# Another order of the same steps in the per-turn programs of four engines, in a transformer block pipelined over sequence groups

## The chip, the cores and the metric

One core of one Trainium2 chip runs the whole model as one program. The metric is the device time of one execution in microseconds (us). TensorE (PE), VectorE (DVE), ScalarE (ACT) and GpSimd (POOL) each run their own instruction stream in its written order, SyncE (SP) issues the transfers, and semaphores tie the five together.

## The reference

The input x is 32 sequences of 64 tokens with 256 features; a context of the same shape goes with it. Four layers follow each other: L0, a small attention over channels; L1 and L2, transformer layers; L3, a recurrence with a gated feed-forward part. The change lies in the program of L1 and L2. Cut to what matters, one of these two layers is:

```python
def layer(x, enc, self_mask, cross_mask, ...):         # x: (32, 64, 256), 16 heads of 16
    h = layernorm(x, ln1_s, ln1_b)
    q, k, v = split_heads(h @ w_qkv + b_qkv)
    x = x + merge(attention(q, k, v, self_mask)) @ w_ao + b_ao
    h = layernorm(x, ln2_s, ln2_b)
    q = split_heads(h @ w_q + b_q);  k, v = split_heads(enc @ w_kv + b_kv)
    x = x + merge(attention(q, k, v, cross_mask)) @ w_co + b_co
    h = layernorm(x, ln3_s, ln3_b)
    return x + gelu(h @ w1 + b1) @ w2 + b2             # w1: 256x1024

def attention(q, k, v, mask):
    s = einsum(q, k) / 4 * mask - 10000 * (1 - mask)
    return einsum(softmax(s), v)
```

## The kernel before

The program has three phases, one after the other: `phase_a` computes L0, `phase_b` L1 and L2, `phase_c` L3. Everything is float32. The 2048 tokens are cut into 4 groups of 512 tokens (8 sequences), and a group into 4 tiles of 128 tokens (2 sequences on the 128 partitions).

`phase_b` is a software pipeline of 8 turns (2 layers x 4 groups), numbered 0 to 7. A turn n has 8 slots: slots 0 to 3 do the self attention of the 4 tiles of group n, slots 4 to 7 their cross attention. Spread over the slots of the same turn lie two more jobs: the MLP of the group before (`prev`), and the first layer norm and the q, k, v projections of the group after (`nxt`). Turn 0 has no `prev`, turn 7 has no `nxt`; turns 1 to 6 have all three and run as a hardware loop. Each engine has a hand-written function `turn(n, prev, nxt)` that lists its steps in order; a step is a small function that first waits for semaphores and then issues its instructions. An engine never runs a later step before an earlier one.

The path of one attention tile k is: `scores` (PE, line 780), `mask` (DVE, 1172: multiply), `add_mask` (POOL, 632), `maximum` (DVE, 1179), `subtract` (DVE, 1184), `exps` (ACT, 1018), `probs_T` (PE, 788: transposes), `copy_pT` (ACT, 1023), `times_v` (PE, 803), `normalize` (DVE, 1190 and 1192), `result_T` (PE, 811), `copy_cT` (ACT, 1028), `out_project` (PE, 824), `residual` (DVE, 1201 to 1208: add, statistics), `inv_std` (POOL, 637), `norm` (DVE, 1213). In slot k an engine works at several tiles: `scores` and `mask` are two tiles ahead, `maximum`, `subtract` and `exps` one tile ahead, `out_project`, `residual` and `norm` one tile behind.

The self-attended tile then becomes a cross query: `norm_T_mid` (PE, 711), `norm_out_mid` (ACT, 995), `queries_mid` (PE, 761) and its copy, also named `queries_mid` (ACT, 1005). In slots 1 to 4 `out_project` of the next tile waits for that copy, for the PSUM bank is the same.

The MLP of `prev`: `norm_T_mlp` (PE, 722), `norm_out(2)` (ACT, 987), eight times `hidden` (PE, 838) with `pre` (DVE, 1226), two `gelu` of 4 chunks each (ACT, 1034), four `mlp_out` (PE, 850) with `result` (DVE, 1220). `hidden` j waits for `pre` j-2, as there are two banks; `gelu(prev, 0)` waits for `pre` 3, `gelu(prev, 1)` for `pre` 7. `norm_T_mlp` waits for the second `values(1)`.

The entry of `nxt`: `stats_in` (DVE, 1135 to 1142), `inv_std_in` (POOL, 641), `norm_in` (DVE, 1148: subtract the mean, times 1/std; this is the centring), `norm_T_in` (PE, 705; it also waits for `pre` 5), `norm_out(0)` (ACT, 987), `queries_in`, `keys_in` (PE, 683; ACT, 1000 and 1011), `values_in` (PE, 693; DVE `values(0)`, 1155). The context keys and values of group n itself are `keys_ctx`, `values_ctx` (PE, 683 and 693), with `keys(1)` on ACT (1011) and `values(1)` on DVE (1155). `keys_ctx` 0 also waits for `ready["middle"]`, which SP gives once the weights of the layer are there; in turn 4 these are the ones of L2. `add_bias` (POOL, 619 and 625) and `add_bias_in` (POOL, 611) add bias rows to the residual stream.

Of the kernel before, what the change touches and what calls it, by code (L numbers as in the profile page):

```python
# [425 lines left out]
def phase_b(nc, io, ps, w, x_mid, ld_b, ld_c, ld_set, zero_ok, a_stored, b_loads, stored, c_loads):  # L426

    ctx = ExitStack()
    with ctx:
# [172 lines left out]
        def _(pool):  # L602
# [3 lines left out]

# [32 lines left out]
            def inv_std_in(n):  # L639
                pool.wait_ge(in_var_ok, NP * n + NP)  # L640
                pool.tensor_tensor(rstd_in[:, :], var_in[:, :], minus_half[:, :], ALU.pow).then_inc(in_rstd_ok, 1)

            def turn(n, prev, nxt):
                for k in range(TILES):
                    if k >= 1:
                        inv_std(n, k - 1)
                    elif prev is not None:
                        inv_std(prev, TILES - 1)
                    if nxt is not None and k == 1:
                        inv_std_in(nxt)  # L650
                    if k + 2 < TILES:
                        add_mask(n, k + 2)
                    elif nxt is not None:
                        add_mask(nxt, k + 2 - TILES)
                    if k >= 2:
                        add_bias(n, k - 2)
                    elif prev is not None:
                        add_bias(prev, TILES - 2 + k)
                    if nxt is not None and 2 <= k < 2 + NP:
                        add_bias_in(nxt, k - 2)  # L660
# [15 lines left out]
        def _(pe):  # L676
# [20 lines left out]
            def norm_T_in(n, prev):  # L697
                if prev is not None:
# [155 lines left out]
            def begin(n, k, prev):  # L854
                probs_T(n, k)
# [5 lines left out]
            def middle(n, k, nxt):  # L861
                times_v(n, k)
# [5 lines left out]
            def end(n, k):  # L868
                if 1 <= k < 1 + NP:
                    norm_T_mid(n, k - 1)  # L870
                result_T(n, k)

            def turn(n, prev, nxt):
                mlp, more = prev is not None, nxt is not None

                begin(n, 0, prev)
                keys_ctx(n, 0, prev)
                middle(n, 0, nxt)
                keys_ctx(n, 1, prev)
                end(n, 0)  # L880
                values_ctx(n, 0)

                begin(n, 1, prev)
                values_ctx(n, 1)
                middle(n, 1, nxt)
                if mlp:
                    norm_T_mlp(prev, n)
                end(n, 1)
                if mlp:
                    hidden(prev, 0)  # L890
                queries_mid(n, 0)

                begin(n, 2, prev)
# [1275 lines left out]
```

## Time and profile before

| | |
|---|---|
| median of 3 runs | 1296.84 us (1296.36 to 1297.08) |
| the profiled execution | 1294.62 us, span 1292.8 us |
| mean granted TensorE clock | 0.952 |
| busy shares of the span | PE 88%, PEld 54%, DVE 67%, ACT 42%, POOL 33% |
| turns of `phase_b` | from 146.0 us (first `probs_T`) to about 861 us |

The span runs from the first to the last instruction. "Idle before" is the time in which an engine did nothing before an instruction, and the name after the arrow is what ended it. A timeline row gives the start, the length, the engine and line, what it writes and reads, and how many instructions are merged in it. The ends of matmuls are modelled, so that a start taken from one row to the next is surer than an end.

### The profile page before, as it was taken

What the parts mean: (1) busy time and instruction counts of PE and PEld (TensorE: products, weight loads), DVE (VectorE), ACT (ScalarE), POOL (GpSimd) and SP (SyncE); (2) the same over time, 40 slices, a digit from 0 to 9 for tenths busy, and PEclk for the clock granted to TensorE, in tenths of its full rate; (3) what the DMA queues carried; (4) which work ended last, traced back from release to release, by engine and by line L of the source; (5) the groups of instructions that cost most, each with busy time, mean ns of one, the idle gap of its engine ahead of it and who ended that gap; (6) DMA issues with size and microseconds to landing.
All of it is one profiled execution on the core that took longest, in us unless ns stands there. A gap on an engine that the chain in (4) does not pass through costs nothing. (4 is left out here: it accounts for less than half of the span.)

```text
span 1292.8 us, 21232 instructions
## 1 busy us (share of the span) xinstructions
PE 1138.4 (88%) x7808; PEld 702.2 (54%) x7808; DVE 872.5 (67%) x1613; ACT 541.0 (42%) x1003; POOL 425.3 (33%) x387
## 2 busy tenths in 40 slices
PE   6985777999999999899899999887898998989976
PEld 4662555667658667567577576665232433523414
DVE  4993676776866866867767767722368686695664
ACT  3552444463564473463564554521213314214222
POOL 2111243343332333342433432410245353263240
PEclk9997889999999999999999999989699998998987
DMA  7120000001002010103001000300000010000100
GB/s 231 57 94 28 5 18 17 22 1 34 20 0 65 20 57 16 32 16 102 0 16 37 0 0 17 121 17 25 24 1 19 1 34 17 8 27 1 33 0 17
DMA packets 37150, 40.51 MB, mean 31 GB/s; under 512 B 8032, under 2 KB 32608, under 8 KB 36848
## 3 DMA queue, kind: packets, MB, share of 16 engines
q1 hardware_dynamic: 36976, 39.81, 9.5%
q8 instruction: 27, 0.44, 0.1%
q14 instruction: 19, 0.16, 0.0%
q0 software_dynamic: 128, 0.10, 0.0%
HBM read 31.52 MB, written 8.39 MB: 31 GB/s over the span
## 5 line engine op out<-in xcount | busy, mean ns | idle before, releaser
L1179 DVE TENSOR_REDUCE b_neg_max<-b_sc 128x16 f32<-128x1024 f32 x64 | 77.8, 1216 | 84.2 <-POOL b_sc L632 83.7
L838 PE MATMUL ps<-b_hT_mlp,wl 128*128 128x512 f32 x256 | 124.5, 614 | 9.9 <-ACT b_hT_mlp L987 8.8
L850 PE MATMUL ps<-w,b_act_g 128*128 128x256 f32 x512 | 119.9, 389 | 6.0 <-ACT b_act_g L1034 5.5
L637 POOL TENSOR_TENSOR b_rstd<-b_var,b_minus_half 128x1 f32<-128x1 f32 x64 | 35.1, 548 | 260.0 <-DVE b_var L1208 260.0
L1538 POOL TENSOR_TENSOR c_rs<-c_st,c_rF 128x512 f32<-128x512 f32 x64 | 82.0, 1284 | 107.7 <-DVE c_st L1956 107.7
L632 POOL TENSOR_TENSOR b_sc<-b_sc,b_self_add 128x1024 f32<-128x1024 f32 x32 | 75.8, 2368 | 104.7 <-DVE b_sc L1172 104.7
L850 PEld LDWEIGHTS ps<-w,b_act_g 128*128 128x128 f32 x512 | 96.8, 194 | 24.5 <-ACT b_act_g L1034 6.4
L1018 ACT ACTIVATE b_sc<-b_sc 128x1024 f32<-128x1024 f32 x64 | 67.9, 1062 | 93.9 <-DVE b_sc L1184 93.3
L632 POOL TENSOR_TENSOR b_sc<-b_sc,b_cross_add 128x1024 f32<-128x1024 f32 x32 | 75.5, 2359 | 82.6 <-DVE b_sc L1172 82.6
L1023 ACT ACTIVATE b_pT<-ps 128x512 f32<-128x512 f32 x128 | 70.2, 604 | 64.1 <-PE ps L788 64.1
L1184 DVE TENSOR_TENSOR b_sc<-b_sc,b_neg_max 128x1024 f32<-128x1024 f32 x64 | 79.2, 1238 | 1.2
L1956 DVE TENSOR_TENSOR_SCAN c_st<-c_decay,ps 128x512 f32<-128x512 f32 x64 | 77.0, 1208 | 0.0
L838 PEld LDWEIGHTS ps<-b_hT_mlp,wl 128*128 128x128 f32 x256 | 45.7, 192 | 57.1 <-issue 42.9
L788 PE MATMUL ps<-ident,b_sc 128*128 128x128 f32 x512 | 70.4, 283 | 6.3 <-ACT b_sc L1018 6.3
L824 PE MATMUL ps<-wl,b_cT 128*128 128x256 f32 x256 | 70.2, 397 | 3.8 <-ACT cross_q L1005 2.4
L1517 POOL TENSOR_TENSOR c_x<-c_x,c_xn 128x512 f32<-128x512 f32 x40 | 49.0, 1245 | 65.4 <-DVE c_x L1932 65.4
L788 PEld LDWEIGHTS ps<-ident,b_sc 128*128 128x128 f32 x512 | 61.4, 146 | 13.1 <-ACT b_sc L1018 6.8
L1624 PE MATMUL ps<-c_vS,area 128*128 128x512 f32 x128 | 64.8, 619 | 4.0 <-DVE c_st L1956 4.0
L1611 PE MATMUL ps<-c_x,area 128*128 128x512 f32 x128 | 66.2, 667 | 0.0
L1220 DVE TENSOR_TENSOR b_x_out<-ps,b_x_mlp 128x256 f32<-128x256 f32 x32 | 13.6, 425 | 75.2 <-PE ps L850 66.9
L683 PE MATMUL ps<-b_hT_in,wl 128*128 128x512 f32 x128 | 62.6, 617 | 1.7 <-ACT b_hT_in L987 1.7
L1226 DVE TENSOR_SCALAR b_act_g<-ps,vl 128x512 f32<-128x512 f32 x64 | 47.7, 746 | 18.5 <-PE ps L838 18.5
(186 smaller groups left out, 2328.9 us busy)
## 6 DMA issues: line engine op xcount, KB each, us to landing
wl<-in_wl SPq DMA_DIRECT2D x4, 1024.0 KB, 6.7
b_x_in<-x_mid SPq DMA_DIRECT2D x8, 512.0 KB, 3.9
enc<-in_ctxT SPq DMA_DIRECT2D x8, 512.0 KB, 3.6
x_mid<-b_x_out SPq DMA_DIRECT2D x8, 512.0 KB, 2.9
area<-in_wc SPq DMA_DIRECT2D x1, 2272.0 KB, 8.2
a_x_in<-in_x SPq DMA_DIRECT2D x16, 128.0 KB, 2.3
a_y_in<-in_ctx SPq DMA_DIRECT2D x16, 128.0 KB, 2.4
w<-in_w SPq DMA_DIRECT2D x2, 1024.0 KB, 9.7
```

The lines of the kernel that those rows point to most:

```text
L632: pool.tensor_tensor(t, t, m.unsqueeze(1).broadcast_to([P, NH, S]), ALU.add).then_inc(add_ok, 1)
L788: mm = pe.transpose(ps[:, PT + half, i * P:(i + 1) * P], sc[:, k % 2, half, 2 * i:2 * i + 2, :].rearrange("q i k -> q (i k)"), w["ident"][ ...
L824: mm = pe.matmul(ps[:, CO, OUT], cT[:, half, p * P:(p + 1) * P], weight(("ao", "co")[a], half), start=(half == 0), stop=(half == 1))
L838: mm = pe.matmul(ps[:, YB + j % 2, :], weight("w1", k, j * P, (j + 1) * P), hT_mlp[:, k, :], start=(k == 0), stop=(k == NC - 1))
L850: mm = pe.matmul(ps[:, YB + MLP_BANK[p], 0:D], act_g[:, j, p * P:(p + 1) * P], w["w2"][:, j, :], start=(j == 0), stop=(j == NJ - 1))
L1018: act.activation(t, t, ACT.Exp).then_inc(exp_ok, 1)
L1023: act.activation(pT[:, b, :, :].rearrange("k i q -> k (i q)"), ps[:, PT + b, :], ACT.Copy).then_inc(pT_ok, 1)
L1179: dve.tensor_reduce(neg_max[:, k % 2, :], t, AX, ALU.max, negate=True).then_inc(max_ok, 1)
L1184: dve.tensor_tensor(t, t, neg_max[:, k % 2, :].unsqueeze(2).broadcast_to([P, 2 * NPAIR, S]), ALU.add).then_inc(sub_ok, 1)
L1538: pool.tensor_tensor(rs[:, i % 4, :], st[:, i % 3, :], rF[:, i // RS, :], ALU.mult).then_inc(rs_ok, 1)
L1611: mm = pe.matmul(ps[:, PROJ + m % 2, :], weight(name, k, c * P, (c + 1) * P), x5[:, j % 2, k, :], start=(k == 0), stop=(k == NC - 1))
L1956: dve.tensor_tensor_scan(st[:, i % 3, :], decay[:, i // RS, :, :].rearrange("f b t -> f (b t)"), ps[:, VB[i % 4], :], 0.0, ALU.mult, ALU.a ...
```

## The change

In every one of the four `turn` functions the steps stay the same and their order changes. (The tests `if mlp` and `if more` become `if n is None: return` within the steps, and `begin`, `middle`, `end` of PE and `end` of ACT are written out; this issues nothing else.) "..." stands for parts in which the order stays.

VectorE:
```diff
                 next_mask(n, 0, nxt)
                 cross_masks(n)
+                values(1, n, 0)
 
                 next_maximum(n, 1, nxt)
-                values(1, n, 0)
+                last_residual(n, 1, prev)
                 next_subtract(n, 1, nxt)
-                last_residual(n, 1, prev)
                 values(1, n, 1)
                 normalize(n, 1)
                 last_norm(n, 1, prev)
                 next_mask(n, 1, nxt)
                 stats_in(nxt)
+                pre(prev, 0)
+                last_residual(n, 2, prev)
 
                 next_maximum(n, 2, nxt)
-                pre(prev, 0)
+                norm_in(nxt)
                 next_subtract(n, 2, nxt)
-                last_residual(n, 2, prev)
                 pre(prev, 1)
                 normalize(n, 2)
                 last_norm(n, 2, prev)
                 next_mask(n, 2, nxt)
                 pre(prev, 2)
-                norm_in(nxt)
 
                 next_maximum(n, 3, nxt)
+                last_residual(n, 3, prev)
                 pre(prev, 3)
                 next_subtract(n, 3, nxt)
-                last_residual(n, 3, prev)
                 pre(prev, 4)
...
                 next_maximum(n, 6, nxt)
-                pre(prev, 7)
                 next_subtract(n, 6, nxt)
+                pre(prev, 7)
                 last_residual(n, 6, prev)
                 last_norm(n, 6, prev)
-                values(0, nxt, 0)
                 normalize(n, 6)
                 next_mask(n, 6, nxt)
+                values(0, nxt, 0)
                 result(prev, 0)
```
(`last_residual(n, k)` is `residual` of tile k-1, `next_maximum(n, k)` is `maximum` of tile k+1, `next_mask(n, k)` is `mask` of tile k+2; so with the others.)

TensorE, written out:
```diff
                 probs_T(n, 0); last_project(n, 0, prev)
+                times_v(n, 0)
                 keys_ctx(n, 0, prev)
-                times_v(n, 0)
                 next_scores(n, 0, nxt)
...
                 values_ctx(n, 1)
+                next_scores(n, 1, nxt)
                 times_v(n, 1)
-                next_scores(n, 1, nxt)
                 norm_T_mlp(prev, n)
...
                 times_v(n, 2); next_scores(n, 2, nxt)
                 hidden(prev, 2, nxt)
+                hidden(prev, 3, nxt)
                 norm_T_mid(n, 1); result_T(n, 2)
-                hidden(prev, 3, nxt)
                 queries_mid(n, 1)
 
                 probs_T(n, 3); last_project(n, 3, prev)
-                hidden(prev, 4, nxt)
                 times_v(n, 3)
+                hidden(prev, 4, nxt)
                 next_scores(n, 3, nxt)
...
                 values_in(nxt, 1, prev)
                 times_v(n, 7)
+                mlp_out(prev, 2, nxt)
                 next_scores(n, 7, nxt)
-                mlp_out(prev, 2, nxt)
                 result_T(n, 7)
```

ScalarE:
```diff
                 copy_pT(n, 0)
+                keys(1, n, 0)
                 next_exps(n, 0, nxt)
-                keys(1, n, 0)
                 copy_cT(n, 0)
...
                 copy_cT(n, 3)
-                norm_out(0, nxt)
                 queries_mid(n, 2)
+                norm_out(0, nxt)
                 copy_pT(n, 4)
                 queries_in(nxt, 0)
                 next_exps(n, 4, nxt)
-                queries_in(nxt, 1)
                 norm_out_mid(n, 3); copy_cT(n, 4)
+                queries_in(nxt, 1)
                 queries_mid(n, 3)
```

GpSimd: `add_bias(prev, 6)` moves from behind `add_mask` in slot 0 to behind `inv_std` in slot 1, `add_bias(n, 0)` from slot 2 (behind `add_mask`) to the end of slot 1, and `add_bias_in(nxt, 2)` in slot 4 from the end to before `add_mask`:
```diff
+                last_inv_std(n, 1, prev)
+                add_bias(prev, 6)
+                inv_std_in(nxt)
+                next_add_mask(n, 1, nxt)
+                add_bias(prev, 7)
+                add_bias(n, 0)
+
+                last_inv_std(n, 2, prev)
+                next_add_mask(n, 2, nxt)
+                add_bias_in(nxt, 0)
```

## Rows read from the trace of the kernel before

**Rows 1.** The page's first part: engine, busy us, share of the span, instructions.
```profile
PE 1138.4 (88%) x7808; PEld 702.2 (54%) x7808; DVE 872.5 (67%) x1613; ACT 541.0 (42%) x1003; POOL 425.3 (33%) x387
```

**Rows 2.** Busy times by stretch, one turn: length, then PE, PEld, DVE, ACT, POOL, clock.
```profile
320.00:411.40 91.40, 87.16 (x802) 61.78 (x801) 66.14 (x127) 48.20 (x76) 32.62 (x29) 1.00 0.10 30
```

**Rows 3.** Timeline of PE, turn 2: start, length, engine, line, tiles, count [idle before].
```profile
336.16 1.09 PE L722 MATMUL ps<-ident,b_xc 128*128 128x128 f32 x8 [0.64 <-DVE cross_v L1155]
...
338.85 1.98 PE L838 MATMUL ps<-b_hT_mlp,wl 128*128 128x512 f32 x4 [1.04 <-ACT b_hT_mlp L987]
...
349.64 0.44 PE L711 MATMUL ps<-ident,b_xc 128*128 128x128 f32 x2 [0.36 <-DVE b_xc L1213]
...
360.93 0.44 PE L711 MATMUL ps<-ident,b_xc 128*128 128x128 f32 x2 [0.46 <-DVE b_xc L1213]
...
362.80 1.09 PE L705 MATMUL ps<-ident,b_xc_in 128*128 128x128 f32 x8 [1.21 <-DVE b_act_g L1226]
363.72 1.06 PE L761 MATMUL ps<-b_hT_mid,wl 128*128 128x128 f32 x8
...
366.00 1.13 PE L824 MATMUL ps<-wl,b_cT 128*128 128x256 f32 x4 [0.35 <-ACT cross_q L1005]
...
427.56 1.09 PE L722 MATMUL ps<-ident,b_xc 128*128 128x128 f32 x8 [0.64 <-DVE cross_v L1155]
```

**Rows 4.** Timeline of DVE, slots 2 to 4 of the same turn.
```profile
343.73 1.22 DVE L1179 TENSOR_REDUCE b_neg_max<-b_sc 128x16 f32<-128x1024 f32 x1 [3.45 <-POOL b_sc L632]
...
346.66 0.42 DVE L1201 TENSOR_TENSOR b_x_cur<-ps,b_x_res 128x256 f32<-128x256 f32 x1
...
347.89 0.75 DVE L1226 TENSOR_SCALAR b_act_g<-ps,vl 128x512 f32<-128x512 f32 x1
...
351.30 3.81 DVE L1148 TENSOR_SCALAR b_xc_in<-b_x_in,b_mv_in,b_rstd_in 128x256 f32<-128x256 f32 x4
...
356.81 1.21 DVE L1184 TENSOR_TENSOR b_sc<-b_sc,b_neg_max 128x1024 f32<-128x1024 f32 x1
...
367.32 0.42 DVE L1201 TENSOR_TENSOR b_x_cur<-ps,b_x_res 128x256 f32<-128x256 f32 x1 [0.37 <-PE ps L824]
```

**Rows 5.** Timeline of POOL beside it.
```profile
350.80 2.36 POOL L632 TENSOR_TENSOR b_sc<-b_sc,b_cross_add 128x1024 f32<-128x1024 f32 x1 [2.23 <-DVE b_sc L1172]
```

**Rows 6.** The tile `b_xc_in`, all of `norm_in`: ns shortest/median/longest, first and last start.
```profile
L1148 DVE TENSOR_SCALAR b_xc_in<-b_x_in,b_mv_in,b_rstd_in x32: 401/814/2445, 113.6 to 722.5; 128x256 f32<-128x256 f32 x32
```

**Rows 7.** Timeline of ACT, slot 3 of turn 2.
```profile
358.06 1.06 ACT L1018 ACTIVATE b_sc<-b_sc 128x1024 f32<-128x1024 f32 x1 [3.51 <-DVE b_sc L1184]
...
360.42 1.91 ACT L1034 ACTIVATE b_act_g<-b_act_g 128x2048 f32<-128x2048 f32 x1
362.24 0.79 ACT L995 ACTIVATE b_hT_mid<-ps,vl 128x128 f32<-128x128 f32 x2
```

**Rows 8.** Timelines of PE, DVE and ACT in turn 7.
```profile
812.15 1.13 PE L824 MATMUL ps<-wl,b_cT 128*128 128x256 f32 x4
...
820.11 1.16 PE L761 MATMUL ps<-b_hT_mid,wl 128*128 128x128 f32 x8 [0.68 <-ACT b_hT_mid L995]
...
841.45 2.07 PE L850 MATMUL ps<-w,b_act_g 128*128 128x256 f32 x4 [2.72 <-ACT b_act_g L1034]
...
812.10 1.22 DVE L1184 TENSOR_TENSOR b_sc<-b_sc,b_neg_max 128x1024 f32<-128x1024 f32 x1
...
838.71 0.74 DVE L1226 TENSOR_SCALAR b_act_g<-ps,vl 128x512 f32<-128x512 f32 x1
...
815.72 1.91 ACT L1034 ACTIVATE b_act_g<-b_act_g 128x2048 f32<-128x2048 f32 x1
...
839.48 1.91 ACT L1034 ACTIVATE b_act_g<-b_act_g 128x2048 f32<-128x2048 f32 x1 [0.69 <-DVE b_act_g L1226]
```

**Rows 9.** Timelines of DVE and PE in slot 6 of turn 0.
```profile
213.45 1.38 DVE L1155 TENSOR_TENSOR area<-ps,rl 64x512 f32<-64x512 f32 x2
...
215.63 0.69 PE L811 MATMUL ps<-ident,b_c_tok 128*128 128x128 f32 x2 [3.00 <-DVE b_c_tok L1192]
```

**Rows 10.** Timeline of PE in slot 0 of turn 4.
```profile
506.78 1.98 PE L683 MATMUL ps<-enc,wl 128*128 128x512 f32 x4 [2.00 <-SPq L532]
508.69 1.13 PE L803 MATMUL ps<-area,b_pT 128*64 128x34 f32 x32
```

More of the change, by code:

```diff
@@ L639, in inv_std_in, with last_inv_std @@
             def inv_std_in(n):
+                if n is None:
+                    return
                 pool.wait_ge(in_var_ok, NP * n + NP)
                 pool.tensor_tensor(rstd_in[:, :], var_in[:, :], minus_half[:, :], ALU.pow).then_inc(in_rstd_ok, 1)
-            def turn(n, prev, nxt):
[L644 to L660, printed above, removed]
+            def last_inv_std(n, k, prev):
+                if k >= 1:
+                    inv_std(n, k - 1)
+                elif prev is not None:
+                    inv_std(prev, TILES - 1)
@@ L866, in middle @@
                     scores(nxt, k + 2 - TILES)
[L868 to L871, printed above, removed]
             def turn(n, prev, nxt):
-                mlp, more = prev is not None, nxt is not None
-                begin(n, 0, prev)
+                probs_T(n, 0)
+                last_project(n, 0, prev)
+                times_v(n, 0)
                 keys_ctx(n, 0, prev)
-                middle(n, 0, nxt)
+                next_scores(n, 0, nxt)
@@ L879, in turn @@
                 keys_ctx(n, 1, prev)
[L880 removed]
+                result_T(n, 0)
                 values_ctx(n, 0)
[L883 removed]
+                probs_T(n, 1)
+                last_project(n, 1, prev)
                 values_ctx(n, 1)
[L885 to L890, printed above, removed]
[L891 to L893 removed]
@@ L946, in turn @@
-                begin(n, 7, prev)
-                if more:
-                    values_in(nxt, 1, prev)
-                middle(n, 7, nxt)
-                if mlp:
-                    mlp_out(prev, 2, nxt)
-                end(n, 7)
-                if mlp:
-                    mlp_out(prev, 3, nxt)
+                next_scores(n, 1, nxt)
+                times_v(n, 1)
+                norm_T_mlp(prev, n)
+                norm_T_mid(n, 0)
+                result_T(n, 1)
+                hidden(prev, 0, nxt)
@@ new lines, in turn @@
+                next_scores(n, 3, nxt)
+                hidden(prev, 5, nxt)
+                norm_T_mid(n, 2)
+                result_T(n, 3)
+                norm_T_in(nxt, prev)
+                queries_mid(n, 2)
+                probs_T(n, 4)
+                last_project(n, 4, prev)
+                queries_in(nxt, 0)
+                times_v(n, 4)
+                next_scores(n, 4, nxt)
+                queries_in(nxt, 1)
+                norm_T_mid(n, 3)
+                result_T(n, 4)
+                keys_in(nxt, 0)
@@ L1057, in turn @@
                 next_exps(n, 1, nxt)
-                if mlp:
-                    norm_out(2, prev)
-                end(n, 1)
+                norm_out(2, prev)
+                norm_out_mid(n, 0)
+                copy_cT(n, 1)
                 queries_mid(n, 0)
```

229 lines of the change are left out of this document (127 added, 102 removed).

## The prediction

> **What bounds the kernel now.** I read the page's shares first: PE is busy for 88% of the span, DVE for 67% [rows 1]. The chain of waits that ended last says nothing on the changed part, since it reaches back only to the start of the third phase; so I went on to busy times by stretch. A full turn lasts 91.40 us, PE works 87.16 us of it at full clock, DVE 66.14 us [rows 2]. The turns 1 to 6 repeat this nearly to the hundredth, so that one turn, read instruction by instruction, stands for six. In its timeline PE has these gaps: 0.64 before `norm_T_mlp` (waits for `values` on DVE), 1.04 before the first `hidden` (ACT), 0.36 and 0.46 before two `norm_T_mid` (DVE), 1.21 before `norm_T_in` (DVE, `pre` 5), 0.35 before an `out_project` (ACT) [rows 3]. Together 4.06 us: that is all an order can win in a turn. Half of it, 0.36 + 0.46 + 1.21 = 2.03, is DVE being late in slots 2 and 3. There DVE first stands still for 3.45 us until GpSimd has added a mask, and then works without a break, `norm_in` with 3.81 us among it [rows 4]. That `norm_in` runs beside GpSimd's `add_mask` [rows 5]; the shortest of its instructions elsewhere takes 0.401 us [rows 6], so that four would take about 1.4 to 1.6 alone.
>
> So the change relieves DVE where DVE is late. What matters is what PE and ACT then wait for. I follow one full turn (turn 2, starting at 320.1) on its own clock, a step's length being the distance of starts in the rows.
>
> **Slots 0 and 1: +0.35 per turn.** `values(1, n, 0)` comes before `maximum` and must now wait for its matmuls, where before `maximum` filled that time: the second `values(1)`, for which `norm_T_mlp` waits, ends about 0.2 later. `times_v` in front of `keys_ctx` starts without cover behind `out_project`; `copy_pT` is done by then, and I take 0.15 for the drain (`out_project` takes 1.03 to 1.13 by its rows, depending on what follows [rows 3, 8]; bounds 0 and 0.3). `keys(1)` before `exps` on ACT has 1 us of slack to `probs_T`: nothing. `scores` before `times_v` only gives `copy_pT` time. `norm_T_mlp` starts at 336.5 instead of 336.16, and its wait for ACT, 1.04, stays.
>
> **Slot 2: +0.7 more.** `residual` of tile 1 is now before `maximum`. It needs `out_project`, which PE starts at 342.8 (0.35 late), and it can start 1.32 after that (366.00 to 367.32 [rows 3, 4]): 344.1. With its statistics it takes 1.23 (346.66 to 347.89 [rows 4]), so `maximum` starts at 345.3 instead of 343.73. Then `norm_in`, GpSimd being idle by then: 1.4, instead of 3.81 later on. `subtract` follows at 347.8, `pre` 1 at 349.0 (347.89 before), and `hidden` 3, moved ahead of `norm_T_mid`, waits for that `pre`: 0.15 on PE. The old wait of 0.36 before `norm_T_mid` is gone, for DVE now has the time of `hidden` 3. But `hidden` 3 had a second use: it covered ACT's `norm_out_mid`, for which `queries_mid` waits. Turn 7 shows the same two steps without cover: 0.68 idle [rows 8], and the matmuls after an idle start some 0.1 later each. Sum: 0.35 - 0.36 + 0.15 + 0.68 + 0.2 = +1.0; `queries_mid` of tile 1 starts at about 352.9, where it was 351.9.
>
> **Slot 3: back to about +0.5.** `out_project` of tile 2 starts at 354.8, `residual` of tile 2 (now before `pre` 3 and `subtract`) at 356.0, `pre` 3 at 357.25, `subtract` at 357.9. Before, `subtract` was at 356.81 [rows 4] although `norm_in` was in the way. From here two chains go on. DVE's: `pre` 5 is done early enough for `norm_T_in` at 362.7, before 362.80. ACT's: `subtract` to `exps` 1.25, `exps` to `gelu` 2.36 (a table load between), `gelu` to `norm_out_mid` 1.82 (356.81, 358.06, 360.42, 362.24 [rows 4, 7]), and 0.86 to `queries_mid` on PE, by turn 7. That makes 357.9 + 6.3 = 364.2, where PE had come to it at 363.72 [rows 3]. So ACT takes the place of DVE: the 1.21 before `norm_T_in` shrinks, a new wait stands behind it, and the net is +0.5. On ACT, `queries_mid` before `norm_out(0)` takes away the 0.35 before `out_project`, but `norm_out(0)`, 1.45 us of work, then ends later and `queries_in` on PE waits: +0.5 stays.
>
> **Slots 4 to 7: nothing in a full turn.** No PE gap there hangs on DVE. `pre` 7 is one `subtract` (1.2) later; `gelu` 1 has a table load of 1.3 in front of it that does not wait for `pre` (in turn 7 the load is done and the `gelu` still waits 0.69 [rows 8]), so it is hidden. `scores` behind `mlp_out` 2 is 3.6 us later, but the `maximum` it leads to comes after `result` 3 anyway; GpSimd's mask is ready 0.7 us before. If that cover is gone, each 0.1 goes onto the next turn's `exps`, which has 1 us of slack. The GpSimd moves fall into its idle time; what they feed is needed a slot later. SP's waits are met in the same slots as before.
>
> A full turn: +0.5, six of them +3.0. Bounds: from -1.5 (the 2.03 and the 0.35 won, the 0.68 and 0.2 lost) to +1.2 (all of slot 2 stays).
>
> **Turn 7: +4.0, once.** It has no `norm_in`, so DVE was not the bound, and nothing is relieved. `residual` of tile 1 still moves in front of `maximum`, and the exposed 0.68 is there too: `out_project` of tile 2 at 813.5 instead of 812.15 [rows 8]. `residual` in front of `subtract` then costs it in full: 813.5 + 1.24, + 1.23, + 0.66 puts `subtract` at 816.6 instead of 812.10, `gelu` (3.62 after it by the rows) at 820.2 instead of 815.72, and `queries_mid` of tile 2 at 820.2 + 1.8 + 0.86 = 822.9 instead of 820.11 [rows 8]: +2.8. In slot 6 `gelu` hangs on `pre` 7 with its load already done (838.71 to 839.48 to 841.45 [rows 8]), and `subtract` in front adds 1.2 to a wait that PE has in full. 2.8 + 1.2 = +4.0; bounds 2.5 and 5.
>
> **Turn 0: -1.4.** PE waits 3.00 us in slot 6 for `normalize`, in front of which stood `values(0)` with 1.41 [rows 9]; it now stands behind. The next wait hangs on the same chain, so the gain is kept. Bounds -2.5 and +0.5 (its early part is as unsure as slots 0 to 3 are). **Turn 4: -1.0.** `keys_ctx` waits 2.00 us for a weight load's mark [rows 10], and `times_v` now runs in that time. Bounds -1.1 and -0.5.
>
> **Sum.** 3.0 + 4.0 - 1.4 - 1.0 = +4.6 us. On the profiled execution: 1294.62 + 4.6 = 1299.2 (1292.8 span). The runs shown lie 2.2 us above that execution, so against their median of 1296.84: 1301.4.
>
> **A rule against the trace.** The row shows `norm_in` at 3.81 us beside a GpSimd instruction that kept its usual 2.36 [rows 4, 5]. The Trainium skill, SBUF — State Buffer, "Who interferes with whom", says that such an operation of VectorE and one of GpSimd exclude each other for a whole instruction, and that the order of issue decides who waits. By that rule the trace agrees, and the moved GpSimd additions, `add_bias(prev, 7)` and `add_bias(n, 0)`, which now end just before `norm_in`, could hold it up. What that would cost is the third rival.
>
> **Rivals.**
> 1. *The relief reaches PE* (faster). If `subtract` of slot 3 comes by 357.0, ACT's chain ends before PE is free, and the DVE gaps go: -2.03 - 0.35 + 0.68 + 0.2 = -1.5 per turn, -9.0 in six, with the other turns (+1.6) -7.4: 1289.4. For it: `norm_in` alone gives back 2.4 us of DVE, and 3.45 us of idle get filled. Against: `residual` 2 waits for PE's `out_project`, which no DVE time makes earlier. The point is 0.9 us of `subtract`'s start. Chance 0.2.
> 2. *Wins and losses cancel* (no change). If the full turn comes out at 0 (drains smaller, `queries_mid` gap smaller), +1.6 is left: 1298.4. For it: each step is a few tenths, as the errors are. Chance 0.23.
> 3. *The new places collide* (clearly slower). GpSimd's two additions of 0.7 us slip into `norm_in` or into the statistics before it, and `maximum` and `subtract` go 0.7 later on a chain that has no slack: 6 x 0.7 = 4.2 more, 1305.6. The clock speaks for some of it too: turn 7 gets idle times over 2 us on PE. Chance 0.12.
> 4. *The order does not do what it says*, a step being ordered by its semaphores anyway: true for GpSimd's moves, not for DVE's, where the waits come in program order. It falls under rival 2.
>
> **How the numbers follow.** Forecast 0.45 at 1301.4; its own range is 1299.4 to 1304. A difference of 0.2% (2.6 us) is what a measurement can tell from none: below 1294.2 is faster, above 1299.4 slower. Slower: 0.45 + 0.12 = 0.57; same 0.23; faster 0.20. The range 1292 to 1306 leaves out most of rival 1 and the tail of rival 3, some 0.2 in all.
>
> **What would show it.** A full turn of 91.9 us (91.4 before), with gaps before `queries_mid` (L761 <- L995) in slots 2 and 3, none over 0.2 before `norm_T_mid`, a smaller one before `norm_T_in`, none before the `out_project` of slot 4; `norm_in` near 1.5 us; in turn 7 `queries_mid` of tile 2 some 43.6 us after the turn's start instead of 40.8, and a wait of about 4 us before the first `mlp_out`; in turn 4 a gap of about 1 us. I am wrong if the full turn falls below 91.2: then ACT's chain does not bound slot 3.

## The result and the profile after

| | kernel before | changed kernel | ratio, 95% interval |
|---|---|---|---|
| four runs each | 1296.96 us (1296.36 to 1297.55) | 1308.06 us (1306.85 to 1309.37) | 1.0082 [1.0069, 1.0095] |
| repeated with e9, 11 and 5 runs | 1297.51 us (1294.27 to 1298.62) | 1307.18 us (1307.02 to 1309.23) | 1.0079 [1.0066, 1.0092] |
| profiled execution, span | 1292.8 us | 1305.3 us | |

The order is slower, as forecast, but by about 10 us where 4.6 were forecast, and 1308.06 lies above the upper end of the range, 1306. On the page PE is busy for 15.3 us more and DVE for 13.8 us less [rows 1]:

```profile
PE 1153.7 (88%) x7808; PEld 703.4 (54%) x7808; DVE 858.7 (66%) x1613; ACT 540.5 (41%) x1003; POOL 433.1 (33%) x387
```

The count of instructions is the same, so the same matmuls took longer. A lower clock does that, and the mean granted clock is 0.945 instead of 0.952; but it is not all, as a full turn shows. One turn from the view by windows (length, then PE, PEld, DVE, ACT, POOL, clock), against [rows 2]:

```profile
321.64:413.82 92.18, 88.32 (x803) 61.57 (x802) 64.00 (x128) 48.13 (x76) 33.48 (x30) 1.00 0.09 30
```

The clock is at its full 2.4 GHz throughout. The turn is 0.78 us longer and DVE works 2.14 less in it. PE stands idle for 3.86 instead of 4.24, and is busy 1.16 longer: six such turns hold 7 of the 15.3 us, at full clock. The timeline of PE in this turn (start, length, engine, line, tiles, count [idle before]) answers to [rows 3]. L763 is `norm_T_mlp`, L887 `hidden`, L750 `norm_T_mid`, L808 `queries_mid`, L744 `norm_T_in`, L720 `queries_in`:

```profile
337.90 1.09 PE L763 MATMUL ps<-ident,b_xc 128*128 128x128 f32 x8 [0.71 <-DVE cross_v L1201]
...
340.59 1.98 PE L887 MATMUL ps<-b_hT_mlp,wl 128*128 128x512 f32 x4 [1.03 <-ACT b_hT_mlp L1031]
...
349.04 4.03 PE L887 MATMUL ps<-b_hT_mlp,wl 128*128 128x512 f32 x8
352.90 0.38 PE L750 MATMUL ps<-ident,b_xc 128*128 128x128 f32 x2
...
354.18 1.16 PE L808 MATMUL ps<-b_hT_mid,wl 128*128 128x128 f32 x8 [0.68 <-ACT b_hT_mid L1039]
...
364.05 1.09 PE L744 MATMUL ps<-ident,b_xc_in 128*128 128x128 f32 x8 [0.52 <-DVE b_act_g L1276]
365.59 1.16 PE L808 MATMUL ps<-b_hT_mid,wl 128*128 128x128 f32 x8 [0.45 <-ACT b_hT_mid L1039]
...
368.80 1.98 PE L720 MATMUL ps<-b_hT_in,wl 128*128 128x512 f32 x4 [0.21 <-ACT b_hT_in L1031]
```

Both waits for DVE before `norm_T_mid` are gone, its wait before `norm_T_in` shrank from 1.21 to 0.52, and the 0.35 before `out_project` went too. In their place stand 0.68, 0.45 and 0.21, all for ACT. A part of the added busy time is a wait that the rows do not show as one: the eight matmuls of `hidden` 2 and 3, now in one row with no gap, take 4.03, and 3.70 in turn 7, where `norm_in` is missing and `pre` 1, for which `hidden` 3 waits, comes earlier. DVE's timeline shows where its time went, against [rows 4] (L1247 `residual`, L1192 `norm_in`, L1230 `subtract`):

```profile
345.52 0.42 DVE L1247 TENSOR_TENSOR b_x_cur<-ps,b_x_res 128x256 f32<-128x256 f32 x1 [2.16 <-PE ps L871]
...
347.86 1.37 DVE L1192 TENSOR_SCALAR b_xc_in<-b_x_in,b_mv_in,b_rstd_in 128x256 f32<-128x256 f32 x4
...
357.40 0.42 DVE L1247 TENSOR_TENSOR b_x_cur<-ps,b_x_res 128x256 f32<-128x256 f32 x1 [0.61 <-PE ps L871]
...
359.31 1.22 DVE L1230 TENSOR_TENSOR b_sc<-b_sc,b_neg_max 128x1024 f32<-128x1024 f32 x1
```

`norm_in` takes 1.37 instead of 3.81, and `subtract` in slot 3 still comes later in the turn than before: 37.92 us behind the turn's first `probs_T` (321.39) instead of 36.74 (320.07). ACT's chain from there, against [rows 7]:

```profile
360.56 1.06 ACT L1066 ACTIVATE b_sc<-b_sc 128x1024 f32<-128x1024 f32 x1 [3.58 <-DVE b_sc L1230]
...
362.93 1.91 ACT L1084 ACTIVATE b_act_g<-b_act_g 128x2048 f32<-128x2048 f32 x1
364.74 0.79 ACT L1039 ACTIVATE b_hT_mid<-ps,vl 128x128 f32<-128x128 f32 x2
```

To see where the spans differ I cut all traces at the same steps: the first `probs_T` of turn 0, the `norm_T_mlp` of each turn, the first `mlp_out` of turn 7, and the first transpose of the third phase.

| us | turn 0 to `norm_T_mlp` of 1 | full turn | six of them, with turn 4 | turn 7 to `mlp_out` | sum of the three stretches | last phase |
|---|---|---|---|---|---|---|
| before | 98.72 | 91.40 | 550.51 | 46.19 | 695.42 | 386.54 |
| before, profiled again (e8) | 98.48 | 91.40 | 550.54 | 46.20 | 695.22 | 389.54 |
| changed | 100.45 | 92.18 | 554.05 | 49.68 | 704.18 | 389.49 |
| changed, profiled again (e9) | 100.32 | 92.16 | 553.91 | 49.65 | 703.88 | 389.52 |

The part that the diff touches costs 8.76 us (8.66 in the repetition): 1.73 in turn 0, 3.54 in the six turns, 3.49 in turn 7. The rest of the 12.5 us between the two spans lies outside these stretches; e8 and e9 below take it up.

### The profile page after: what moved, and what is told of

The parts are those of the page before. It is cut to its first block and busy times, and to the rows that moved or that the text cites. A ratio compares the mean times of both kernels' runs of the same rounds, so it can differ in the third digit from the quotient of the medians.

```text
span 1305.3 us, 21232 instructions
## 1 busy us (share of the span) xinstructions
PE 1153.7 (88%) x7808; PEld 703.4 (54%) x7808; DVE 858.7 (66%) x1613; ACT 540.5 (41%) x1003; POOL 433.1 (33%) x387
## 5 line engine op out<-in xcount | busy, mean ns | idle before, releaser
L887 PE MATMUL ps<-b_hT_mlp,wl 128*128 128x512 f32 x256 | 126.8, 624 | 10.3 <-ACT b_hT_mlp L1031 8.8
L640 POOL TENSOR_TENSOR b_rstd<-b_var,b_minus_half 128x1 f32<-128x1 f32 x64 | 43.4, 678 | 212.3 <-DVE b_var L1254 211.9
L1230 DVE TENSOR_TENSOR b_sc<-b_sc,b_neg_max 128x1024 f32<-128x1024 f32 x64 | 79.2, 1238 | 1.2
L887 PEld LDWEIGHTS ps<-b_hT_mlp,wl 128*128 128x128 f32 x256 | 45.7, 193 | 63.6 <-issue 43.9
L1658 PE MATMUL ps<-c_vS,area 128*128 128x512 f32 x128 | 64.8, 619 | 4.0 <-DVE c_st L1990 4.0
L1218 DVE TENSOR_TENSOR b_sc<-ps,b_self_mul 128x1024 f32<-128x1024 f32 x32 | 39.1, 1222 | 44.4 <-PE ps L827 43.6
L720 PE MATMUL ps<-b_hT_in,wl 128*128 128x512 f32 x128 | 63.0, 620 | 3.3 <-ACT b_hT_in L1031 3.3
```

Source lines behind the costliest of these rows:

```text
L887: mm = pe.matmul(ps[:, YB + j % 2, :], weight("w1", k, j * P, (j + 1) * P), hT_mlp[:, k, :], start=(k == 0), stop=(k == NC - 1))
L1230: dve.tensor_tensor(t, t, neg_max[:, k % 2, :].unsqueeze(2).broadcast_to([P, 2 * NPAIR, S]), ALU.add).then_inc(sub_ok, 1)
```

## The experiments

Undoing a part is done on the changed kernel (e1, e2, e3, e5, e6), doing a part alone on the kernel before (e4, e11, e7, e10). The lengths that a trace gives repeat to 0.02 us for a turn and to 0.24 for turn 0, so one profile decides what a single time could not. A "full turn" runs from the `norm_T_mlp` of turn 2 to that of turn 3. Three profiles (e1, e10, e11) have a stretch of 3.4 us at the lower clock within the turns where the others have none; it is told with e11 and e10.

**e1, the residuals of tiles 1 and 2 back behind `subtract`.**

```
                 pre(prev, 0)
-                last_residual(n, 2, prev)
...
                 next_subtract(n, 2, nxt)
+                last_residual(n, 2, prev)
...
                 next_maximum(n, 3, nxt)
-                last_residual(n, 3, prev)
                 pre(prev, 3)
                 next_subtract(n, 3, nxt)
+                last_residual(n, 3, prev)
```

> The changed kernel with VectorE's residual of tiles 1 and 2 back behind subtract (slots 2 and 3). Theory A (residual in front of subtract holds up ScalarE's chain exps, gelu, norm_out_mid): a full turn falls from 92.18 us to about 91.2, the 0.45 wait before queries_mid of tile 2 and the 0.21 before queries_in go, the 0.68 wait before queries_mid of tile 1 stays; in turn 7 the 1.84 wait falls to 0.68, and the whole is some 8 to 9 us faster than the changed kernel (about 1299). Rival B (the order of PE alone is to blame, the exposed queries_mid): the turn stays above 91.9. Rival C (the granted clock in the tail and in the last phase makes a third of the loss, whatever the order): the time behind the first phase-C transpose stays at 389.5 us and does not go back to 386.6.

Measured: full turn 91.46, 0.72 less than the changed kernel; turn 7 49.12 to `mlp_out`; 1300.84 us (kernel before, same chip: 1299.32). PE's waits in slots 2 and 3:

```profile
353.65 1.16 PE L808 MATMUL ps<-b_hT_mid,wl 128*128 128x128 f32 x8 [0.68 <-ACT b_hT_mid L1039]
...
363.49 1.09 PE L744 MATMUL ps<-ident,b_xc_in 128*128 128x128 f32 x8 [0.48 <-DVE b_act_g L1276]
...
367.52 1.99 PE L720 MATMUL ps<-b_hT_in,wl 128*128 128x512 f32 x4 [0.21 <-ACT b_hT_in L1031]
```

The 0.45 before `queries_mid` of tile 2 is gone. The 0.21 before `queries_in`, which I expected to go with it, stays, and the turn is 0.26 longer than I expected. The last phase stays at 389.6, as rival C had it. The residuals in front are the largest single item of a full turn. Turn 7 gave back only 0.56: the 1.84 before `queries_mid` of tile 2 is 0.68 there now, but `norm_T_mid` of tile 3 waits 1.01 for DVE where it waited 0.38.

**e2, `hidden` 3 back between `result_T` and `queries_mid`.**

```
                 hidden(prev, 2, nxt)
-                hidden(prev, 3, nxt)
                 norm_T_mid(n, 1)
                 result_T(n, 2)
+                hidden(prev, 3, nxt)
                 queries_mid(n, 1)
```

> The changed kernel with hidden 3 back behind result_T in slot 2 of PE. Theory A: the 0.68 wait before queries_mid of tile 1 goes, 0.1 to 0.4 before norm_T_mid comes back, and out_project of tile 2, residual, subtract and gelu all come about 0.6 earlier, so a full turn is 91.5 to 91.7; turn 7 is some 1 us shorter. Rival B (this move is the whole loss): the turn falls to 91.4 or below. Rival D (VectorE bounds the slot anyway): the turn stays at 92.1.

Measured: full turn 92.12, only 0.06 less, as rival D said; turn 7 48.74, 0.94 less, as theory A said; 1306.12 us. In the full turn the gap did not go, it moved to the step before:

```profile
354.38 0.44 PE L750 MATMUL ps<-ident,b_xc 128*128 128x128 f32 x2 [1.00 <-DVE b_xc L1259]
```

`norm` of tile 1 is late by that much, and `hidden` 3 was hiding it. The cause is `norm_in` in front of it: e3, with the residual back too, has the same wait. So in a full turn my 0.68 "exposed by `hidden` 3" is a real gap but not a cost of that move. In turn 7, which has no `norm_in`, it is one.

**e3, both back.** The edits of e1 and e2 together.

> Both moves undone, the rest of the change kept (centring behind maximum, values, times_v, GpSimd and ScalarE moves). Theory A: the two losses add up, a full turn is 90.6 to 91.0, below the 91.40 of the kernel before, turn 7 as before or 1 us longer (pre 7 behind subtract), and the whole is 1293 to 1297. Rival B: the remaining moves lose as well and the turn stays at or above 91.4.

Measured: full turn 91.40, turn 7 48.20, 1300.91 us. The turn is exactly that of the kernel before; I had expected a gain of 0.4 to 0.8, and rival B (the remaining moves lose as well) holds. The wait before `norm_T_mid` is 1.0 here too. That alone does not use up the gain: e7 below has `norm_in` in the same place, with the same wait, and a turn of 90.62. The 0.78 between e7 and e3 lie where only the order of the rest differs: 0.42 in slots 0 and 1 (0.22 of it `times_v`, by e5), 0.2 between `out_project` and `scores` in slot 3, where PE does `times_v` before `hidden` 4 (4.03 us against 3.84), and 0.15 in slot 7 (0.14 by e6). The 0.2 had no term in the forecast. No run moves that pair alone.

**e4, the centring alone, on the kernel before.**

```
                 next_maximum(n, 2, nxt)
+                if more:
+                    norm_in(nxt)
...
                     pre(prev, 2)
-                if more:
-                    norm_in(nxt)
```

> The kernel before with only norm_in moved, from the end of slot 2 to behind maximum in the same slot. Theory A: its four instructions take about 1.5 us instead of 3.8 (GpSimd idle beside them), but pre 1, normalize and norm of tile 1 come 1.3 later, so that norm_T_mid of tile 1 waits 1.7 instead of 0.36; a full turn is 91.3 to 91.5, as before. Rival E (the centring itself is the gain or the loss of the change): the turn moves by more than 0.4 either way.

Measured: full turn 91.29, turn 7 unchanged (46.19), 1299.50 us. PE's waits for DVE in slots 2 and 3:

```profile
352.03 0.44 PE L711 MATMUL ps<-ident,b_xc 128*128 128x128 f32 x2 [1.66 <-DVE b_xc L1213]
...
363.77 1.09 PE L705 MATMUL ps<-ident,b_xc_in 128*128 128x128 f32 x8 [0.48 <-DVE b_act_g L1226]
```

Against [rows 3], waits of 0.46 and 0.73 are won in slot 3 and 1.30 is lost in slot 2. That would be 0.11 more, but the turn is 0.11 shorter: where a wait is gone the steps also follow each other closer. From `norm_T_mid` of tile 1 to that of tile 2 it takes 0.62 less, and the wait is only 0.46 of that. A cheaper `norm_in` does help, but behind `maximum` it stands in front of the `norm` that PE needs next.

**e5, `times_v` back behind `keys_ctx` in slot 0.**

```
                 last_project(n, 0, prev)
-                times_v(n, 0)
                 keys_ctx(n, 0, prev)
+                times_v(n, 0)
                 next_scores(n, 0, nxt)
```

> The changed kernel with times_v of slot 0 back behind keys_ctx 0 on PE. From the first probs_T of turn 0 to the first norm_T_mlp of turn 1 it took 98.72 us before and 100.45 in the changed kernel. Theory F (in turn 0 this move meets PE at its slow clock, which then rises later, so that the same work up to scores 2 takes 1.36 more): the stretch falls to about 99.1; a full turn loses 0.1 to 0.2 of its 92.18; turn 3 to 4 goes from 93.19 to about 94.1, since the wait for the weights' mark has no cover. Rival G (what turn 0 lost comes from the order of VectorE in slots 1 to 3): the stretch stays at 100.3 or more.

Measured: full turn 91.96 (0.22 less), step from turn 3 to 4 94.23 (the 2.0 wait of [rows 10] is back), 1305.47 us. Turn 0 came as the surprise: 97.16 instead of 100.45, 3.3 less, where I had expected 99.1. Rival G is out. The timelines of PE from the first `probs_T` on, the changed kernel first (L850 `times_v`, L720 `keys_ctx`, L827 `scores`), then this one:

```profile
145.25 1.97 PE L835 MATMUL ps<-ident,b_sc 128*128 128x128 f32 x8 [6.32 <-ACT b_sc L1066]
147.16 1.93 PE L850 MATMUL ps<-area,b_pT 128*64 128x34 f32 x32
149.01 3.78 PE L720 MATMUL ps<-enc,wl 128*128 128x512 f32 x4
152.72 1.22 PE L827 MATMUL ps<-area 64*64 64x256 f32 x16
153.87 1.98 PE L720 MATMUL ps<-enc,wl 128*128 128x512 f32 x4
```

```profile
147.10 1.97 PE L835 MATMUL ps<-ident,b_sc 128*128 128x128 f32 x8 [6.32 <-ACT b_sc L1066]
148.86 3.14 PE L720 MATMUL ps<-enc,wl 128*128 128x512 f32 x4
151.94 1.13 PE L850 MATMUL ps<-area,b_pT 128*64 128x34 f32 x32
152.99 1.09 PE L827 MATMUL ps<-area 64*64 64x256 f32 x16
154.02 1.99 PE L720 MATMUL ps<-enc,wl 128*128 128x512 f32 x4
```

The same four steps take 8.62 us in the one and 6.92 in the other. `times_v` takes 1.93 in front and 1.13 behind, the first `keys_ctx` 3.78 and 3.14 (the second 1.98, at full clock). The stretch of 2 us in which the clock leaves 1.2 GHz, the changed kernel first:

```profile
152.00:154.00 2.00, 2.00 (x18) 0.72 (x18) 0.00 (x0) 1.17 (x2) 0.00 (x0) 0.74 0.00 0
```

```profile
150.00:152.00 2.00, 2.00 (x5) 0.46 (x6) 0.00 (x0) 0.00 (x0) 0.00 (x0) 0.65 0.00 0
```

If 0.74 and 0.65 are each a part at 0.5 and the rest at 1.0, the clock rose at 153.0 and 151.4: 7.8 and 4.3 us behind the first `probs_T`. In the kernel before, whose window from 150 to 152 has 0.81, it was 4.7. The clock of all thirteen traces divides the same way: it rises 7.6 to 7.8 us behind the first `probs_T` in the six with `times_v` in front, and 4.0 to 4.7 us behind it in the other seven. The windows of the first two parts of turn 0 (to `norm_T_mid` of tile 0, then to that of tile 2) say the same, the changed kernel first:

```profile
145.25:165.54 20.29, 18.59 (x190) 12.56 (x190) 12.99 (x21) 9.91 (x15) 3.84 (x2) 0.81 0.11 34
165.54:187.56 22.02, 15.62 (x144) 12.73 (x145) 14.27 (x40) 7.83 (x16) 9.10 (x7) 0.77 0.01 1
```

```profile
147.10:165.69 18.59, 16.88 (x190) 11.75 (x191) 13.00 (x21) 10.01 (x15) 3.84 (x2) 0.88 0.13 37
165.69:186.55 20.86, 13.60 (x144) 10.87 (x145) 14.37 (x40) 7.60 (x16) 9.04 (x7) 0.84 0.00 2
```

The granted clock is 0.81 and 0.77 instead of 0.88 and 0.84, PE is busy 1.7 and 2.0 us longer with the same matmuls, and the two parts last 1.70 and 1.16 longer. In the kernel before the two parts are 18.54 and 21.25 long. The six profiles with `times_v` in front (the two of the changed kernel, e1, e2, e3, e6) have 100.1 to 100.5 in turn 0; none without it is over 98.8.

**e6, slots 6 and 7 back.**

```
-                mlp_out(prev, 2, nxt)
                 next_scores(n, 7, nxt)
+                mlp_out(prev, 2, nxt)
...
-                next_subtract(n, 6, nxt)
                 pre(prev, 7)
+                next_subtract(n, 6, nxt)
```

> The changed kernel with pre 7 back in front of subtract (slot 6, VectorE) and scores back in front of mlp_out 2 (slot 7, PE). Theory A: in turn 7 the first mlp_out comes 1.2 us earlier (48.4 instead of 49.7 behind norm_T_mlp), since gelu has its table loaded and only waits for pre 7; a full turn is 0.1 to 0.15 shorter by the drain between matmuls of different shape in slot 7 (92.05). Rival H (pre 7 bounds a full turn too): the full turn falls by 0.5 or more. Rival I (turn 7 hangs on the weights or on slot 3 alone): its mlp_out stays at 49.7.

Measured: full turn 92.04 (0.14 less), turn 7 48.45 (1.23 less), 1303.58 us. As expected: `pre` 7 behind one `subtract` costs one `subtract`, once, in the turn that has nothing to hide it. The wait before `mlp_out` is 2.74 instead of 3.97.

**e11, the residuals in front alone, on the kernel before.**

```
+                last_residual(n, 2, prev)
                 next_maximum(n, 2, nxt)
...
                 next_subtract(n, 2, nxt)
-                last_residual(n, 2, prev)
...
                 next_maximum(n, 3, nxt)
+                last_residual(n, 3, prev)
...
                 next_subtract(n, 3, nxt)
-                last_residual(n, 3, prev)
```

> The kernel before with one part of the change only: residual of tile 1 in front of maximum in slot 2, residual of tile 2 in front of pre 3 and subtract in slot 3. Theory A: subtract of slot 3 comes 1.2 later, and with it exps, gelu, norm_out_mid and, behind norm_out(0), ScalarE's queries_mid: queries_mid on PE waits some 0.5 and the out_project behind it 0.8 to 1.0; a full turn is 92.4 to 92.8 (91.40 before), turn 7 longer by 1.5. Rival N (in front or behind, residual is the same work, VectorE has the time): the full turn stays within 0.2 of 91.4.

Measured: full turn 91.86 (0.46 more than before), turn 7 49.27 (3.1 more), 1302.17 us. The turn lost half of what I expected. The new wait takes in part the place of another: `queries_mid` of tile 2 is 0.61 late, and the `out_project` behind it, which waited 0.35 before, gets 0.15 of that back:

```profile
363.38 1.09 PE L705 MATMUL ps<-ident,b_xc_in 128*128 128x128 f32 x8 [1.21 <-DVE b_act_g L1226]
364.91 1.16 PE L761 MATMUL ps<-b_hT_mid,wl 128*128 128x128 f32 x8 [0.45 <-ACT b_hT_mid L995]
```

In turn 7, DVE's timeline shows how the moved step costs. Before, `maximum` could run in this hole; now it stands behind a `residual` that waits for PE:

```profile
806.91 0.42 DVE L1201 TENSOR_TENSOR b_x_cur<-ps,b_x_res 128x256 f32<-128x256 f32 x1 [5.31 <-PE ps L824]
...
808.12 1.21 DVE L1179 TENSOR_REDUCE b_neg_max<-b_sc 128x16 f32<-128x1024 f32 x1
```

But not all of the 3.1 is its price. `queries_mid` of tile 2 comes 26.63 us behind `norm_T_mlp` instead of 24.85: 1.78 are lost there, near the 1.5 expected. The other 1.30 come behind it, where the order is that of the kernel before, and the window says why:

```profile
827.30:830.70 3.40, 3.40 (x18) 2.56 (x18) 1.57 (x3) 3.09 (x6) 0.00 (x0) 0.50 1.01 365
```

No other profile but e1's has the lower clock within turn 7 ahead of its last wait, and in e1 the wait before `mlp_out` takes it up (2.42 instead of 3.97). Turn 5 to 6 of e11 has such a stretch too, 93.14 us against 91.86. Whether it belongs to this order or to the execution one profile cannot tell.

**e8 and e9, the two kernels again, unchanged.** The diff between them is the one of the document.

> The kernel before, unchanged, profiled once more. Theory C (the 389.5 us of the last phase and the slow second pair of mlp_out belong to the execution, not to the order): the last phase takes 389.5 here too, where the first profile had 386.5, and the rest is as in that profile. Rival K (the order of phase B sets the clock of what follows): it is 386.5 again and the slow stretch of the tail is missing.

> The changed kernel, unchanged, beside the kernel before on one chip. The difference of phase B between the profiles (first probs_T to the first mlp_out of turn 7) is 704.2 - 695.3 = 8.9 us. Theory C (nothing outside phase B changed; the 386.5 us of the last phase in the first profile of the kernel before was that execution's): the two medians differ by 9 us, ratio 1.0069 (1.006 to 1.008). Rival K (the slower phase B also makes the clock in the last phase worse, 2 us more): 11 us, ratio 1.0085 or more.

Measured: the third phase, which no edit touches, lasts 386.54 us in the first profile of the kernel before and 389.54 in the second. One 10 us window at the same place of it in the first and second profile of the kernel before, and in the changed kernel:

```profile
936.30:946.30 10.00, 10.00 (x23) 3.64 (x22) 2.90 (x5) 2.39 (x4) 2.71 (x3) 1.00 0.00 0
```

```profile
937.70:947.70 10.00, 10.00 (x21) 3.76 (x20) 1.50 (x2) 2.39 (x4) 2.31 (x2) 0.87 0.00 0
```

```profile
945.80:955.80 10.00, 10.00 (x21) 3.76 (x20) 1.50 (x2) 2.39 (x4) 2.32 (x2) 0.87 0.00 0
```

The second and third agree, clock included. In all thirteen profiles this phase has one of two lengths: 386.5 to 386.9 (before, e10, e11) or 389.5 to 389.65 (the other ten), and both kinds of order are in the second group. The last `mlp_out`s ahead of that phase behave likewise: 7.69 us in four profiles, 9.2 to 9.3 in the others. Of the 12.5 us between the two spans, 8.8 are of the order, 2.95 are the last phase's, of which e8 shows that they come without a change of code, and the first `probs_T` came 0.8 earlier. The 1.56 left lie between the first `mlp_out` of turn 7 and the last phase, and whose they are is open. The repeated pair has 1.55 there as well (66.50 against 64.95 us), though its last `mlp_out`s agree. Yet e4, which is the kernel before from turn 7 on, has 66.2, and e1 and e6, which are most of the changed order, have 64.8 and 65.0.

The times of many runs differ by 11.1 and 9.7 us. 8.7 us would be a ratio of 1.0067, at the lower edge of both intervals, and with the 1.55 it is 1.0079, so 1.0 to 2.4 us more may still be the order's. Both ratios that were named for e9 lie in its interval, so it did not tell them apart. Whether the order makes the longer phase more frequent stays open: neither profile of the full changed order is in the short group; e10 and e11, which hold parts of the change, are.

**e7 and e10, what is good, alone.** On the kernel before: `pre` 0 to the end of slot 1, `values(0)` behind `normalize` in slot 6, on ACT `queries_mid` of tile 2 before `norm_out(0)`; `norm_in` behind `maximum` (e7) or behind `norm` of tile 1 (e10). The part that differs, in e10:

```
                 last_norm(n, 2, prev)
+                if more:
+                    norm_in(nxt)
                 next_mask(n, 2, nxt)
...
                     pre(prev, 2)
-                if more:
-                    norm_in(nxt)
```

> The kernel before with four moves only: norm_in behind maximum in slot 2, pre 0 at the end of slot 1 (in the 3.45 us in which VectorE waits for GpSimd), values(0) behind normalize and mask in slot 6, and ScalarE's queries_mid in front of norm_out(0) in slot 3. The residuals stay behind subtract. Theory A: in a full turn pre 5 ends 0.7 earlier and norm_T_in with it, a full turn is 90.7 to 90.8 instead of 91.40; turn 0 gains 1.4 by slot 6; turn 7 stays within 0.3. Sum 6 x 0.65 + 1.4 = some 5 us faster than the kernel before, ratio 0.996. Rival J (VectorE is late whatever comes first, what norm_in gives is lost before norm_T_mid of tile 1): the full turn stays at 91.3 as with the centring alone, ratio 0.999.

> As the picked version (e7), with norm_in not behind maximum but behind norm of tile 1, in front of mask, in slot 2. Theory L (in the picked version PE's 1.0 wait before norm_T_mid of tile 1 is there because norm_in stands before subtract, pre 1, normalize and norm): that wait goes, mask of tile 4 keeps its time, norm_T_in is then bound by pre 5 again with a wait of about 0.9, and a full turn falls from 90.6 to 90.2 or 90.3; ratio to the kernel before 0.993. Rival M (PE only waits elsewhere, at norm_T_in, as much longer): the full turn stays at 90.6, ratio 0.995.

Measured: e7 1290.84 us, ratio 0.9948 [0.9934, 0.9961], full turn 90.62; e10 1289.44 us, ratio 0.9940 [0.9925, 0.9954], full turn 90.32. Both beat both kernels. The intervals of e7 and e10 overlap, so which of them is the better is told by the turns alone, and not by all of them: where the weights of turn 4 are awaited, e10's trace has the lower clock for 3.4 us (`keys_ctx` takes 3.66 us, 1.98 in e7), the step from turn 3 to 4 is 1.70 longer for it, and the six turns together are 545.7 against 545.8. Turn 0 is 96.9 and 96.8, turn 7 46.2. DVE of e10, and its PE: no wait is left before `norm_T_mid` of tile 1, for `norm_in` now stands just behind `norm`, on which that transpose waits, and still ahead of the `mask` that sets GpSimd to work. The 1.21 before `norm_T_in` is back, where 0.9 was expected.

```profile
347.37 0.40 DVE L1213 TENSOR_SCALAR b_xc<-b_x_cur,b_mv,b_rstd 128x256 f32<-128x256 f32 x1
347.69 1.38 DVE L1148 TENSOR_SCALAR b_xc_in<-b_x_in,b_mv_in,b_rstd_in 128x256 f32<-128x256 f32 x4
348.99 1.22 DVE L1172 TENSOR_TENSOR b_sc<-ps,b_cross_mul 128x1024 f32<-128x1024 f32 x1
```

```profile
347.83 0.44 PE L711 MATMUL ps<-ident,b_xc 128*128 128x128 f32 x2
...
360.47 1.09 PE L705 MATMUL ps<-ident,b_xc_in 128*128 128x128 f32 x8 [1.21 <-DVE b_act_g L1226]
```

With e7 the full turn's +0.78 can be walked through, one kernel at a time: before 91.40, e7 90.62 (-0.78, four moves); e3 91.40 (+0.78, the rest of the change but the residuals and `hidden` 3); e1 91.46 (+0.06, `hidden` 3); changed 92.18 (+0.72, the residuals).

## Why the prediction was right in direction and wrong in size

*Slots 0 to 3 of a full turn: right.* Measured from the turn's first `probs_T` (forecast behind it): `norm_T_mlp` +0.42 (+0.35), `residual` of tile 1 at 24.13 (24.0), `queries_mid` of tile 1 at 32.79 (32.8), `subtract` of slot 3 at 37.92 (37.8), `queries_mid` of tile 2 at 44.20 (44.1), `queries_in` +0.51 (+0.5). The claim that ACT takes DVE's place is what the traces show: 0.68, 0.45 and 0.21 for ACT, and e1 takes the 0.45 away with the residuals. The attribution within it was half wrong: `hidden` 3 got the blame for 0.68, but e2 shows that putting it back exposes 1.00 of DVE instead.

*"Slots 4 to 7: nothing in a full turn": wrong by 0.27.* Six turns cost 3.54 with turn 4's gain in them, where 2.0 was forecast. e6 finds 0.14 of the 0.27 in slots 6 and 7; the way from `queries_in`, which now waits, to `times_v` is another 0.1 (1.91 us against 1.81). Two terms of 0.1 or so, taken as nothing, are 1.6 us when they come six times.

*Turn 4: right.* The wait of 2.00 is now 0.95, and the step from turn 3 to 4 is 1.24 less beyond a full turn's +0.78 (forecast 1.0):

```profile
509.66 1.98 PE L720 MATMUL ps<-enc,wl 128*128 128x512 f32 x4 [0.95 <-SPq L532]
```

*Turn 7: right.* +3.49 behind `norm_T_mlp`, where 4.0 less its 0.35 was forecast. PE's timeline, against [rows 8], has `queries_mid` of tile 2 43.6 us behind the turn's start (forecast 43.6), and the wait of about 4 us:

```profile
826.90 1.16 PE L808 MATMUL ps<-b_hT_mid,wl 128*128 128x128 f32 x8 [1.84 <-ACT b_hT_mid L1039]
...
849.43 5.35 PE L901 MATMUL ps<-w,b_act_g 128*128 128x256 f32 x16 [3.97 <-ACT b_act_g L1084]
```

The terms hold too. The 1.2 for `pre` 7 is 1.23 in e6. The 2.8 for `queries_mid` of tile 2 is 2.78: 0.48 from slots 0 and 1, 0.94 from `hidden` 3 in front (e2; e3 against e1 has 0.92), and 1.36 left for the residuals, which cost 1.78 alone (e11) and of which e1 gives back 1.16 at that step. But e1 gives back only 0.56 at `mlp_out`, for with the residuals back `norm_T_mid` of tile 3 waits longer for DVE.

*Turn 0: the step that failed.* The forecast had -1.4 from `normalize` moved in front of `values(0)`, and the early part at nothing: `times_v` in front of `keys_ctx`, "0.15 for the drain" in a loop turn, had no price of its own in turn 0. The first half holds: the wait of 3.00 [rows 9] is 1.57 after, and e7 and e10, which make that move without `times_v`'s, have 96.9 and 96.8 against 98.5 to 98.7. The second does not. Turn 0 starts after PE has stood idle for 6.32 us, at a granted clock of 0.50, the 1.2 GHz level, and the clock rises 7.8 us behind the first `probs_T` instead of 4.7. Everything until then is slower, slots 1 to 3 get a lower clock too, and the move costs 3.3 us, as e5 shows. The bounds for that term (-2.5 to +0.5) let the early part vary by the errors of a loop turn. They leave out the clock, which in the profile before is granted at 0.50 for the first 4.7 us of turn 0. +1.73 measured against -1.05 forecast (with turn 1's 0.35) is 2.8 of the 4.2 us that the stretches missed by; the six turns are 1.5 of it. Why the clock rises later with this order is not settled: e5 shows that the one exchange brings it and takes it away, and no run took that apart further.

*The profiled execution.* The forecast was laid on a single execution that had a short last phase. It was set against the median by adding 2.2 us for both kernels alike, which is right if the order does not touch what lies outside the changed turns. Against the median the forecast missed by 6.7 us (1308.06 against 1301.4). That is about 2.4 more than by the stretches, and in the repetition it is 1.0 more. That part of the miss stays open.

*The rivals.* The relief reaches PE: not with this order, since `residual` 2 waited for PE as said against it; it does with four of the moves alone and the residuals left where they were (e10, -1.08 a turn). Wins and losses do not cancel, at +0.78 a turn. The new places collide: GpSimd's additions end at 346.8, a microsecond ahead of `norm_in`, and nothing of the 0.7 that this rival had happened. The time is as high as this rival's for another reason.

## What to carry to other kernels

Moving a step forward on an in-order engine moves its wait too: price it by when its input comes, and ask what now stands behind that wait (here `maximum` and `subtract`, on which ACT's whole chain hangs). A step that is slowed by a neighbour engine wants a place where that engine is silent, but behind the step that the bound engine needs next: the same `norm_in` a few instructions later is 0.3 us a full turn better (e10 against e7). An order that is written once but runs in a first, a loop and a last turn has three prices; the first and the last turn here cost 1.7 and 3.5 us, six loop turns 3.5 together, and the first must be read with the clock granted there.

## What the runs showed of the hardware

- Four centring instructions take 1.37 us with GpSimd silent and 3.81 beside its work. The mask addition is not all of that, as the prediction had it: in turn 2 before, the first of the four takes 2.02 us and ends 0.2 us behind the mask addition, the next two take 0.82 and 0.81 beside two bias additions of 0.79 and 0.77 us, and the last, alone again, 0.40. The tile's row, all 32 of them, ns shortest/median/longest, against [rows 6]:

```profile
L1192 DVE TENSOR_SCALAR b_xc_in<-b_x_in,b_mv_in,b_rstd_in x32: 403/406/815, 113.2 to 718.6; 128x256 f32<-128x256 f32 x32
```

- It works the other way too. GpSimd's `inv_std` of one column takes 0.55 us in 55 of 64 places in the changed kernel, and 1.46 in 9, once in each turn and twice in turn 0, as here where DVE has just begun `subtract`, with both inputs in SBUF; the rows of GpSimd and DVE:

```profile
335.42 1.46 POOL L640 TENSOR_TENSOR b_rstd<-b_var,b_minus_half 128x1 f32<-128x1 f32 x1 [4.38 <-DVE b_var L1254]
```

```profile
335.25 1.22 DVE L1230 TENSOR_TENSOR b_sc<-b_sc,b_neg_max 128x1024 f32<-128x1024 f32 x1
```

  The Trainium skill, SBUF — State Buffer, "Who interferes with whom", states that a VectorE instruction with two SBUF inputs contends with a GpSimd instruction that reads SBUF. The trace agrees: GpSimd ended 0.4 us behind `subtract`'s end.
- The same phase of the same program on a different execution took 386.5 or 389.5 us, with a granted clock of 1.00 or 0.87 in the same window. The spans of the two profiles of the kernel before are 1292.8 and 1297.2 us, 4.4 apart with no difference in the code.
